# Roots of the norms on VectorE, four accumulators at the start, another order of the routing, and a 32-bit table in a two-layer mixture-of-experts kernel

## What is computed

```
x = x + blockwise_cumsum(layernorm(x) @ W.T + bias)          # linear, cumsum over 128
x = x + ffn(layernorm(x))                                    # layer 0
x = x + attention(layernorm(x))                              # 16 heads, window 128
x = x + ffn(layernorm(x))                                    # layer 1

ffn(x): xn = layernorm(x) * gamma + beta
        probs = softmax(xn @ router_w.T / 1.5); the top 2 of 8 experts
        out = sum over the two of prob * (silu(xn @ W1[e]) @ W2[e]);  return out + x
```

## Time and profile before

| | |
|---|---|
| median of three executions | 831.33 us |
| profiled execution, its own time | 832.6 us |
| span of that execution | 830.5 us |
| PE busy in the span | 653.1 us, 79% |
| DVE busy | 471.9 us, 57% |
| ACT busy | 324.2 us, 39% |
| POOL busy | 374.4 us, 45% |
| L457, POOL's roots | 32 instructions, 43.3 us busy |
| granted PE clock | 0.906 of full speed on average |

### The profile page before, as it was taken

The page is one execution under the profiler, slowest core; times in us unless marked ns, Lnnn a source line. Parts: engine busy times, 40 slices in busy tenths (PEclk is TensorE's granted clock), DMA queues, the critical chain, the costliest instruction groups (busy, mean ns, idle before and its releaser), DMA issues.

```text
span 830.5 us, 29323 instructions
## 1 busy us (share of the span) xinstructions
PE 653.1 (79%) x11332; PEld 513.4 (62%) x11332; DVE 471.9 (57%) x1716; ACT 324.2 (39%) x536; POOL 374.4 (45%) x384
## 2 busy tenths in 40 slices
PE   4752877899978789898898988677658799888880
PEld 2421676798977546565665656455448688776760
DVE  7867787622235475665757665675876842123224
ACT  3450253232223226465655757366445222222220
POOL 4613583595776300222312100350177677777770
PEclk9865799999989959999999999999856999999995
DMA  7510022122323312021221201010002111224325
GB/s 208 132 38 17 17 55 71 49 68 70 87 73 94 115 34 66 26 78 41 65 63 35 81 16 57 2 42 17 6 20 80 43 52 53 53 79 116 103 63 155
DMA packets 61300, 52.71 MB, mean 63 GB/s; under 512 B 9745, under 2 KB 54674, under 8 KB 61162
## 3 DMA queue, kind: packets, MB, share of 16 engines
q1 hardware_dynamic: 52306, 32.67, 13.5%
q0 software_dynamic: 8864, 18.17, 8.3%
HBM read 30.88 MB, written 19.92 MB: 61 GB/s over the span
## 4 chain that ended last, share of the span: by engine, by line
PE 41%; DVE 24%; issue 13%; POOL 7%; DMA 5%; DVEq 4%; ACT 4%; SPq 0%; POOLq 0%; ACTq 0%
PE stbank L1223 9%; PE bank L1329 4%; POOL xg L507 4%; PE sbank L1287 3%; PE sbank L1282 3%; PE stbank L1313 3%; PE stbank L1213 2%; DVE mx L902 2%; DVE zr L611 2%; DVE xs L859 2%; POOL ytab L514 2%; DMA xg<-table,idx 2%; DVE st L582 2%; PE stbank L1215 2%; PE stbank L1214 2%
## 5 line engine op out<-in xcount | busy, mean ns | idle before, releaser
L1223 PE MATMUL stbank<-wdn,g 128*128 x1136 | 171.4, 296 | 43.1 <-DVE ysb L838 38.7
L507 POOL DMA_INDIRECT xg<-table,idx x142 | 140.5, 989 | 133.4 <-DVE sidx L828 72.3
L994 ACT ACTIVATE g<-stbank 128x512 f32<-128x512 f32 x142 | 84.7, 597 | 263.5 <-PE stbank L1215 263.1
L1223 PEld LDWEIGHTS stbank<-wdn,g 128*128 128x128 f32 x1136 | 145.1, 200 | 61.4 <-issue 52.4
L902 DVE TENSOR_REDUCE mx<-sbank 128x2 f32<-128x320 f32 (+1 forms) x256 | 116.6, 472 | 62.9 <-PE sbank L1287 57.4
L1047 ACT ACTIVATE pT<-stbank 128x1024 f32<-128x1024 f32 (+1 forms) x128 | 116.6, 916 | 71.2 <-PE stbank L1313 70.7
L838 DVE COPY ysb<-stbank 128x128 f32<-128x128 f32 x142 | 41.2, 290 | 172.2 <-PE stbank L1223 110.8
L527 POOL DMA_INDIRECT cg<-yslot,posi x64 | 61.2, 956 | 128.7 <-ACT pT L1047 112.6
L1213 PE MATMUL stbank<-xT,wup 128*128 128x128 f16 x568 | 116.5, 229 | 2.0 <-issue 1.9
L1215 PE MATMUL stbank<-xT,wup 128*128 128x128 f16 x568 | 116.8, 229 | 0.0
L1214 PE MATMUL stbank<-xT,wup 128*128 128x128 f16 x568 | 115.2, 226 | 0.0
(11 more groups left out here) (211 smaller groups left out, 1060.9 us busy)
## 6 DMA issues: line engine op xcount, KB each, us to landing
yslot<-ysb SPq DMA_DIRECT2D x71, 64.0 KB
table<-tb SPq DMA_DIRECT2D x16, 256.0 KB, 2.3
cg<-ytab SPq DMA_DIRECT2D x16, 256.0 KB, 3.6
qz<-dumps SPq DMA_DIRECT2D x96, 32.0 KB
kst<-dumps SPq DMA_DIRECT2D x96, 32.0 KB
xg<-table,idx POOLq DMA_INDIRECT x142
xs<-in_x SPq DMA_DIRECT2D x8, 256.0 KB, 4.9
...
```

Of the source, the lines that this page charges most:

```text
L507: g.indirect_dma_start(xg[:, i % G].rearrange("p a d -> p (a d)"), None, table if t >= FIRST else table[0:CHUNK, :], bass.IndirectOffsetOn ...
L994: a.activation(g32[:, i % 3, :], hbank[i % 2], ACT.Silu, scale=1.0 / WSCALE).then_inc(s_g32, 1)
L1223: ins = mm(ybank, g32[:, i % 3, P * f:P * f + P], w[:, 0, P * f:P * f + P], start=(f == 0), stop=(f == FC - 1))
```

## The change

- **Roots.** POOL's power is gone. `root` on DVE guesses each root from the bits of the number and makes three Newton steps of three instructions. At the start, and for chunk 3, one `root` serves 16 tiles; the attention's norms and chunk 2 have one for each batch.
- **Start.** The linear block of batches 0 to 3 has four accumulators, with the bias matmuls first. All four norms are made before the first sum. The split of the weights (`split_high`, `split_psum`, `split_low`) stands around the routing.
- **Order.** In the passes the two functions `a_step` and `r_step` become `chunk_step` with the steps `Z_AT` and `ROUTE_AT`: layer 0 has its router's norms in steps 8 and 9 and routing steps k = 7 to 17 in s = 12 to 22; layer 1 has them in 0 and 1 and in 4 to 14. The norm's sums and roots of chunk 1's linear block stand before layer 0's pass, those of chunk 3's router before layer 1's.
- **Table.** `table` holds z itself in float32, stored straight from `zr`, which has four buffers. Gamma and beta, and the split in two fp16 parts, are applied after the gather: PE makes one float32 transpose, ACT writes `xa` and the high part of `xT`, DVE the low part as their difference. The rows stay 512 bytes long.

```diff
+MAGIC = float(0x5F3759DF)
+Z_AT = (8, 0)
+ROUTE_AT = (12, 4)
+ROUTE, ROUTED = 7, 17
+ZS = BPC
...
-    table = nc.dram_tensor("table", [B * SEQ, 2 * D], F16).ap()
+    table = nc.dram_tensor("table", [B * SEQ, D], F32).ap()
...
-        zr = sb("zr", [P, 2, TPB, D]); zT = sb("zT", [P, 2, SEQ])
+        zr = sb("zr", [P, ZS, TPB, D]); zT = sb("zT", [P, 2, SEQ])
...
+        xg = sb("xg", [P, G, D]); xa = sb("xa", [P, 2, P]); xT = sb("xT", [P, 3, 2 * P], F16)
...
+        def beside_tiles(layer, s):
+            return [b for b in range(BPC) if max(1, b) == s], [b for b in range(BPC) if Z_AT[layer] + 1 + b // 2 == s], \
+                s - ROUTE_AT[layer] + ROUTE
...
-                elif layer == 0:
-                    a_step(1, s)
-                    r_step(c0 + 1, s - A_BEFORE_R)
                 else:
-                    r_step(c0 + 1, s)
...
+            def rows(cc, i):
+                if i == 0 and cc == CHUNKS:
+                    sp.wait_ge(s_xp, TILES)
+                sp.wait_ge(s_z, z_router(cc, i) + 1)
+                r = CHUNK * (cc % 2) + SEQ * i
+                sp.dma_start(table[r:r + SEQ, :].rearrange("(t p) n -> p t n", p=P),
+                             zr[:, z_router(cc, i) % ZS]).then_inc(s_tbd[i], 16)
...
+                for i in beside_tiles(layer, s)[1]:
+                    rows(CHUNKS * layer + 1, i)
...
-                            pool.wait_ge(s_tbd[k], 16 * 2 * (cc + 1))
+                        for k in range(BPC):
+                            pool.wait_ge(s_tbd[k], 16 * (cc + 1))
...
+            def stats(tile, col):
...
+            def root(c, both):
...
+                var, w = mv[:, c, 1], slice(0, 1 + both)
+                v.tensor_scalar(ve[:, 0, c], var, EPS, None, ALU.add)
                 if both:
...
+                    v.tensor_scalar(ve[:, 1, c], var, 1.0 + EPS, EPS * EPS, ALU.mult, ALU.add)
                 dve.drain()
...
+                v.tensor_scalar(r0[:, w, c].bitcast(I32), ve[:, w, c].bitcast(I32), -0.5, MAGIC, ALU.mult, ALU.add)
+                for to in (r0, r0, rr):
+                    dve.drain()
+                    v.tensor_tensor(newt[:, w, c], r0[:, w, c], r0[:, w, c], ALU.mult)
+                    dve.drain()
+                    v.scalar_tensor_tensor(out=newt[:, w, c], in0=newt[:, w, c], scalar=-0.5, in1=ve[:, w, c],
+                                           op0=ALU.mult, op1=ALU.mult)
+                    dve.drain()
+                    v.scalar_tensor_tensor(out=to[:, w, c], in0=newt[:, w, c], scalar=1.5, in1=r0[:, w, c],
+                                           op0=ALU.add, op1=ALU.mult)
...
+                wait(dve, s_zp, n - ZS + 1)
+                wait(dve, s_tbd[n % ZS], 16 * rows_stored(n - ZS))
...
+            def linear_added(b):
+                dve.wait_ge(s_am, b + 1)
+                v.tensor_tensor(flat(b), flat(b), lbank[b] if b < BPC else bank[1][:, :], ALU.add).then_inc(s_aa, 1)
+                dve.drain()
+            def linear_stats(c):
+                for i in range(BPC):
                     b = BPC * c + i
-                    dve.wait_ge(s_am, b + 1)
-                    v.tensor_tensor(flat(b), flat(b), bank[1][:, :], ALU.add).then_inc(s_aa, 1)
-                    dve.drain()
...
+                    stats(TPB * b, TPB * i)
+                root(slice(0, CT), 0)
+            def linear(c, i):
+                b = BPC * c + i
+                normalise(z_linear(b), TPB * b, TPB * i, 0)
...
+            def router_stats(cc, i):
+                stats(CT * (cc % CHUNKS) + TPB * i, TPB * i)
+            def router_root(cc, cols):
+                root(cols, 1)
...
-                normalise(n, CT * (cc % CHUNKS) + TPB * i, TPB * i, 1)
+            def router(cc, i):
+                normalise(z_router(cc, i), CT * (cc % CHUNKS) + TPB * i, TPB * i, 1)
+            def chunk_step(layer, s):
+                cc = CHUNKS * layer + 1
+                if layer == 0:
+                    for i in range(BPC):
+                        if i // 2 == s:
+                            linear(1, i)
+                        if 3 + i == s:
+                            linear_added(BPC + i)
+                            router_stats(cc, i)
+                    if s == 3 + BPC:
+                        router_root(cc, slice(0, CT))
+                for i in range(BPC):
+                    if Z_AT[layer] + i // 2 == s:
+                        router(cc, i)
+                r_step(cc, s - ROUTE_AT[layer] + ROUTE)
...
-                    dve.wait_ge(s_xp, i + 1)
-                    wait(dve, s_h, i - 2)
-                    v.tensor_copy(xT[:, i % 3, :], xbank[i % 2]).then_inc(s_xt, 1)
+                    dve.wait_ge(s_xa, i + 1)
+                    v.tensor_tensor(xT[:, i % 3, P:2 * P], xa[:, i % 2, :], xT[:, i % 3, 0:P], ALU.subtract).then_inc(s_xt, 1)
...
-                    norm_end(z_attn(b), 0, 0)
+                    root(slice(0, TPB), 0)
...
-            first_router(a_step, r_step)
-            layer_pass(a_step, r_step, x_step, beside, 0)
+            linear_stats(0)
+            for i in range(BPC):
+                linear(0, i)
+            for i in range(BPC):
+                linear_added(i)
+                router_stats(0, i)
+            router_root(0, slice(0, CT))
+            for i in range(BPC):
+                router(0, i)
+            for k in range(ROUTE, ROUTED + 1):
+                r_step(0, k)
+            linear_stats(1)
+            layer_pass(chunk_step, x_step, beside, 0)
...
-                        norm_begin(TPB * norms_at(b, j, 0), TPB * norms_at(b, j, 0), 1)
+                        i = norms_at(b, j, 0)
+                        router_stats(CHUNKS, i)
+                        router_root(CHUNKS, slice(TPB * i, TPB * i + TPB))
...
+            for i in range(BPC):
+                router_stats(CHUNKS + 1, i)
+            router_root(CHUNKS + 1, slice(0, CT))
+            layer_pass(chunk_step, x_step, beside, 1)
...
+            def chunk_step(layer, s):
+                cc = CHUNKS * layer + 1
+                first, second, k = beside_tiles(layer, s)
+                if layer == 0:
+                    for i in first:
+                        evac_z(z_linear(BPC + i))
+                for i in second:
+                    evac_z(z_router(cc, i), True)
+                if 0 <= s - Z_AT[layer] - 3 < BPC:
+                    residual(cc, s - Z_AT[layer] - 3)
                 if k == 8:
...
+                    choices_exp(cc)
...
             def x_step(layer, s):
+                i, _, _ = layer_tile(layer, s)
+                if i is not None:
+                    act.wait_ge(s_xp, i + 1)
+                    wait(act, s_xt, i - 1)
+                    wait(act, s_h, i - 2)
+                    a.activation(xa[:, i % 2, :], xbank[i % 2], ACT.Identity, scale=ga_s[:, 0:1], bias=be_s[:, 0:1])
+                    a.activation(xT[:, i % 3, 0:P], xbank[i % 2], ACT.Identity, scale=ga_s[:, 0:1],
+                                 bias=be_s[:, 0:1]).then_inc(s_xa, 1)
...
-            first_router(a_step, r_step)
+            for i in range(BPC):
+                evac_z(z_linear(i))
+            for e in range(E // 2):
+                split_high(e)
+                if e:
+                    split_low(e - 1)
+            for i in range(BPC):
+                evac_z(z_router(0, i), True)
+            split_low(E // 2 - 1)
+            for e in range(E // 2, E - 2):
+                split_high(e)
+            choices_exp(0)
+            for e in range(E // 2, E):
+                split_low(e)
+                residual(0, e - E // 2)
+                if e + 2 < E:
+                    split_high(e + 2)
...
+            def linear_bias(dst):
+                mm(dst, ones_row[:], cb[:].unsqueeze(1).to_broadcast([1, TPB, D]), start=True, stop=False,
+                   skip_group_check=True)
+            def linear(b):
+                n = z_linear(b)
+                dst = lbank[b] if b < BPC else bank[1][:, :]
+                if b >= BPC:
+                    pe.wait_ge(s_aa, b)
+                    pe.wait_ge(s_idx, 1)
+                    linear_bias(dst)
+                pe.wait_ge(s_zt, n + 1)
+                for t in range(TPB):
+                    ins = mm(dst[:, P * t:P * t + P], zT[:, n % 2, P * t:P * t + P], wc[:], start=False,
+                             stop=True, skip_group_check=True)
+                ins.then_inc(s_am, 1)
+                pe.sem_inc(s_ztf, 1)
...
+            def router_logits(cc, i):
+                if i == 0:
+                    wait(pe, s_lc, cc)
+                ins = logits(cc, i, logits_bank(cc)[:, TPB * i:TPB * i + TPB, :])
+                if i == BPC - 1:
+                    ins.then_inc(s_lg, 1)
+                pe.sem_inc(s_ztf, 1)
...
+            def chunk_step(layer, s):
+                cc = CHUNKS * layer + 1
+                first, second, k = beside_tiles(layer, s)
+                if layer == 0:
+                    if 0 <= s - 2 < BPC:
```

(39 more changed lines are left out.)

237 lines of the change are left out of this document (43 added, 194 removed).

## The result

The changed kernel is slower: 863.23 us (median of four, 856.47 to 866.29) against 830.44 us, a ratio of 1.035 with a 95% interval of 1.030 to 1.040. The ratios in this document are on record for the executions within 1.5% of the fastest of their kernel (all but two of run 8's ten), and are not the quotients of the two medians, which here would be 1.039. On another chip the ratio was 1.0345 (1.027 to 1.042). The prediction was 837 us, range 816 to 848: the measured time lies 15 us above the range. Slower by over 1% had a chance of 0.30. The profiled execution has a span of 862.6 us, 32.1 us more than before.

What follows compares the result with a forecast made beforehand. PE, POOL's pace or waits between engines bound different stretches; PE held 41% of the chain. 832.6 - 10.0 + 5.2 - 1.5 (gather-backs) + 7.3 + 3.5 + 1.0 (subtraction beside POOL) = 838.1 us profiled, so 837 us median, range 816 to 848.

Steps and rivals of the forecast that it cites:

- the price of a root: On DVE: eleven instructions of 0.24 us take 2.7 us, about 3.1 with two lots of 16 columns.
- the rows of a tile: Per tile: ACT's two added copies take 0.8 us, PE's float32 transpose adds nothing; hidden while PE is the bound.
- the attention: DVE roots at batch ends: 1.2 us more per front, with two more fronts and chunk 2: +7.3 us (+4 to +10).
- rival 2: Slower, 848 us: low clock after DVE work at the start of layer 1's pass, more low clock in layer 0; 23%.
- the start: Kernel start to first logits: 38.3 us instead of 48.31, routing unchanged, so -10.0 us.
- chunk 2's norms: In the attention: chunk 2's norms on DVE add 1.2 us, part of the +7.3.
- Last z to logits about 4.4: Last piece of the start: from the last z to the first logits about 4.4 us.
- the prediction's own signs: Forecast wrong if the start gains under 7 us, attention batches keep their period, or tile 25 stands before 150 or after 172.
- lists to tile 25: Layer 0, first lists to tile 25: tile 25 at 160.7 us instead of 165.5; +5.2 us (-12 to +11).
- Layer 1's start: DVE sums and root before tile 0 of layer 1 delay tile 14 by 0 to 8 us; +3.5 taken.
- rival 1: Faster, 817 us: full clock and no waits between lists and tile 25, layer 1's start costs nothing; 28%.
- rival 3: The shared interface, 847 us: DVE's subtraction holds POOL 0.2 us in each of 55 steps, +10 over the sum; 5%.

Runs made afterwards that it cites:

- run 8: Changed kernel with POOL's roots inside the attention, chunk 3's sums and root spread, and chunk 1's ahead of the first routing: 828.6 us, 0.993 of the kernel before.
- run 9: Changed kernel with eight more matmuls at each of six attention batch ends: 853.95 us; the changed kernel as it is, on the same chip: 861.53 us.
- run 7: Changed kernel with POOL's roots everywhere in the attention, the eight fronts and chunk 2's four norms: 843.53 us, 1.012 of the kernel before.
- run 6: Changed kernel with chunk 1's sums and root moved from behind the first routing to ahead of it: 860.43 us, 1.033 of the kernel before.
- run 4: Changed kernel with chunk 3's sums and root spread over steps 0 to 4 of layer 1's pass, norms and routing five steps later: 849.07 us, 1.019.
- run 5: Kernel before, with the DVE root in the attention's eight fronts alone: 847.64 us, 1.017 of the kernel before.
- run 3: Changed kernel with two Newton steps in every root instead of three: 848.07 us, 1.021 of the kernel before.
- run 1: Changed kernel with POOL's roots back in the attention's eight fronts: 847.02 us, 1.018 of the kernel before.
- run 10: Kernel of run 8 with layer 0's second routing one step earlier: 882.84 us, 0.996 of the kernel before, on a slower chip.

## Why the prediction was wrong

**Right: the price of a root.** 11 instructions took 2.7 us, on 32 columns 3.0 (636.38 to 639.36). **Right: the rows of a tile.** ACT's two copies take 0.81 us together (72.33 to 73.14 for tile 0), PE's float32 transpose costs no more than the two before (273 ns, twice 219 ns before that overlap: 5.7 us for 21 tiles in both kernels), and the stretches in which PE or POOL are full kept their pace.

**Wrong in size: the attention, +7.3 predicted, +21.7 measured.** This is the step that failed: "by the rows 1.2 more for each front". It priced DVE's instructions and left the clock where it was, although the first rows of the profile gave it as two-valued, and my own second rival spoke of it for layer 1. What the runs showed in its place, for the five batches: with POOL's roots and full clock they take 179.1 us, 2.3 over before, from the rest of the change and not taken apart; with DVE's roots at full clock 182.5 us, 3.3 more (the eight matmuls' own time included); the changed kernel of run 9 193.6 us, 11.1 more, by the low clock. These are single executions, but the step of 11.1 us has both sides on one chip. The DVE part was, if anything, over-estimated, although the sum counts "two more fronts" as 1.2 us where its own price would make 2.4. For low clock I had 6 us in one rival and none for the attention, and the widest bound (+10) was worked out from instruction times only. With 21.7 in place of 7.3 the sum is 852.5 for the profiled execution, which took 864.4 us; the start (4.5), the lists (2.8), the stretch to the first `back` (2.6, not taken apart) and layer 1 (2.3) make up the rest.

**Wrong in size: chunk 2's norms,** inside that term: 4.8 us for the batch instead of 1.2, and 6.6 to 7.4 in the six other executions. Four roots stand there, and I took one; with POOL's roots the batch was 1.8 us over before in run 7 and not over it in run 8.

**Half right: the start, -10.0 predicted, -5.5 measured.** "Last z to logits about 4.4" took 8.31 us: four transposes, ACT's copy and the products of each batch follow one another, and PE, with little to do, is at half clock from 31 to 48 us. A gain under 7 us at the start was one of the prediction's own signs that it was wrong.

**Right in sign, short: lists to tile 25, +5.2 predicted, +8.0 measured.** The sums and the root behind the lists account for 3.0 us of it (run 6). The rest was not separated. In sum the first 165 us were predicted as -4.8 and came out as +2.5.

**Layer 1's start, +3.5 predicted, within 0 to +8: +5.5 to tile 14.** The 8 us of DVE work ahead of tile 0 were right. The deciding observation of rival 2, the granted clock of the first 30 us, was 0.68, between its two conditions of 0.50 and 1.00, and 0.90 when the work was spread. So rival 2's mechanism was at work in part, and the same mechanism, in another place, was the larger loss. Rival 2's 848 us was the nearest of the four times, and still 15 us short, because it allowed for the clock only at starts of passes.

**The rivals 1 and 3 fall.** The stretch to tile 25 stayed at a clock of 0.86, where rival 1 had full clock. For rival 3, the Trainium skill's "GPSIMD Engine Reference", in its table at the top, has DVE's reads of two SBUF inputs contend with POOL. The trace shows no such hold on POOL's indirect DMAs: they take 972 and 992 ns, 989 and 991 before, and 1.5 us were lost over 56 tiles in all, for a predicted +1.0 and not 11.

The Trainium skill's "TensorE: Matmul & The Clock Gate", section "HAM oscillation — how this bites in real kernels", describes a kernel in which PE waits for a DMA in every round and starts each round at the low clock again. The trace agrees in kind, with 3 to 10 us of half clock behind the ends of batches; PE's waits are 2.2 to 2.8 us here, and for DVE. I had thought of this for the starts of the passes and not asked it of the batch ends.

**What stays open.** Why the clock falls at some batch ends and not at others. At the second to fifth end the profiled executions with the full DVE root before `back` (the changed kernel twice, runs 4, 5 and 6) have PE waiting 2.1 to 2.8 us, and half clock came with all twenty. But at the first end a wait of 2.56 us was followed by none in three of four. Waits of 1.5 to 2.0 us, with POOL's roots or with two Newton steps, were followed by either: 1.51 us by none in the kernel before (three times), by 7 us of half clock once in run 3. Of ten waits of 1.0 to 1.4 us in runs 1, 3, 7, 8 and 10 none was followed by it. With the root one step earlier the waits of 2.45 to 3.45 us, at another instruction, brought half clock at two of four ends. The runs show that the fall is gone when PE is given work there, and not what decides in between.

## What to carry to other kernels

Where PE sets the time and is at full clock, an instruction on another engine that PE waits for is not worth its own length only: ask how long PE then idles, and put the price of half-clock work behind it (here 3.3 us of DVE work and 11.1 us of low clock) into the range. Root-sized chains of small instructions belong where their engine waits anyway (0.49 us of idling in place of 8.31), or in part on an idle engine: with POOL's power DVE's wait and work at a batch's end were some 1.4 us in place of 2.7. Work gathered in one block ahead of a loop costs its length, and the loop may start at the low clock behind it; spread behind the first iterations of layer 1, with the routing later, it gave 11 us back by the last tile.
